# A fused Flamingo block on one core: ternary weights from ScalarE's Sign instead of a clip on VectorE

## The reference, cut to what matters

```
x = x + tanh(g_xattn[0]) * mamba(ctx_1024, layernorm(x))        # selective scan, 16 states
x = x + tanh(g_ffn[0])   * bit_ffn(layernorm(x))                # ternary weights, 512 -> 2048 -> 512
x = x + tanh(g_xattn[1]) * cross_attention(layernorm(x), ctx)   # 16 heads of 128
x = x + tanh(g_ffn[1])   * experts(layernorm(x))                # 4 experts, 512 -> 512 -> 512
```

```
gamma_w = clip(mean(abs(w)), 1e-05, None)
w_dq = clip(round(w / gamma_w), -1.0, 1.0) * gamma_w
```

## Time and profile before

| | us |
|---|---|
| median of 3 runs | 1902.91 |
| lowest, highest | 1902.73, 1903.48 |
| span of the profiled execution | 1906.4 |
| PE busy in it | 1763.0 (92%) |
| DVE busy | 1358.1 (71%) |
| ACT busy | 981.7 (51%) |
| POOL busy | 655.3 (34%) |

### The profile page before, as it was taken

One profiled execution on the slowest core, in us unless ns is written; L12 is line 12 of the kernel. 1 busy time (PEld: TensorE's weight loads), 2 busy tenths in 40 slices (PEclk: granted clock), 3 DMA queues, 4 the chain that ended last, 5 costly groups with the idle time before them and its releaser, 6 DMA issues.

```text
span 1906.4 us, 19429 instructions
## 1 busy us (share of the span) xinstructions
PE 1763.0 (92%) x6054; PEld 803.1 (42%) x6054; DVE 1358.1 (71%) x1963; ACT 981.7 (51%) x1926; POOL 655.3 (34%) x677
## 2 busy tenths in 40 slices
PE   8853999978999999999999999999998989999999
PEld 3321343434444344444443444444444334444543
DVE  2778888899988889989988999897752444431321
ACT  6889665545575455575646465565334333330100
POOL 1222351135565224554632164473202433320100
PEclk9976999989999999999999999999998999999999
DMA  7798992377884115797612368872111699855210
GB/s 256 218 257 232 268 281 71 106 208 186 189 217 121 35 34 127 163 256 198 185 37 54 92 156 234 203 177 78 34 56 45 191 282 268 241 166 214 83 50 34
DMA packets 163175, 300.31 MB, mean 158 GB/s; under 512 B 18937, under 2 KB 51705, under 8 KB 160129
## 3 DMA queue, kind: packets, MB, share of 16 engines
q1 hardware_dynamic: 145792, 236.14, 39.4%
q0 software_dynamic: 17280, 62.92, 16.9%
HBM read 177.64 MB, written 58.33 MB: 124 GB/s over the span
## 4 chain that ended last, share of the span: by engine, by line
PE 64%; DVE 14%; issue 7%; ACT 6%; DMA 4%; POOL 4%; SPq 0%; DVEq 0%; POOLq 0%; ACTq 0%
PE p L781 8%; PE p L792 8%; PE p L758 7%; PE p L741 7%; PE p L828 6%; PE p L634 5%; PE p L720 4%; PE p L715 4%; DVE s_M L957 3%; PE p L843 3%; PE p L764 3%; PE p L681 2%; DVE s_M L952 2%; DVE s_M L962 1%; POOL s_U L1478 1%
## 5 line engine op out<-in xcount | busy, mean ns | idle before, releaser
L957 DVE TENSOR_TENSOR_SCAN s_M<-s_M 128x1024 f32<-128x1024 f32 x128 | 296.7, 2318 | 13.0 <-ACT s_M L1209 10.5
L1100 DVE CUSTOM_DVE_ANT_0 s_U<-p,s_U 128x512 f32<-128x512 f32 x256 | 187.0, 745 | 147.4 <-PE p L758 145.9
L758 PE MATMUL p<-s_U 128*128 128x512 f32 x512 | 268.0, 612 | 4.6 <-DVE s_U L1100 3.4
L1433 POOL DMA_DIRECT2D s_u<-s_M x120 | 112.1, 934 | 463.5 <-DVE s_M L962 418.1
L741 PE MATMUL p<-s_U 128*128 128x512 f32 x512 | 251.8, 600 | 8.3 <-DMA s_U<-in_Wq 3.3
L1478 POOL TENSOR_SCALAR s_U<-s_U 128x512 f32<-128x512 f32 x256 | 242.2, 966 | 6.6
L792 PE MATMUL p<-s_U 128*128 128x512 f32 x512 | 224.3, 593 | 0.0
L781 PE MATMUL p<-s_U 128*128 128x512 f32 x472 | 213.7, 593 | 2.6 <-ACT s_U L1342 2.6
L1209 ACT ACTIVATE s_M<-s_dl,s_small 128x511 f32<-128x511 f32 x256 | 170.4, 716 | 37.2 <-DVE s_M L957 37.1
L1342 ACT COPY s_U<-p 128x512 f32<-128x512 f32 x196 | 105.0, 592 | 162.2 <-PE p L764 160.7
L1337 ACT ACTIVATE s_U<-s_U 128x512 f32<-128x512 f32 x256 | 181.6, 710 | 5.5 <-ACT s_U L1333 0.4
(11 more groups left out here) (178 smaller groups left out, 2424.6 us busy)
## 6 DMA issues: line engine op xcount, KB each, us to landing
s_u<-s_M POOLq DMA_DIRECT2D x120, 512.0 KB, 7.6
s_bc<-bc_scratch SPq DMA_DIRECT2D x128, 256.0 KB, 4.6
k_scratch<-s_U SPq DMA_DIRECT2D x16, 1024.0 KB, 7.0
v_scratch<-s_U SPq DMA_DIRECT2D x16, 1024.0 KB, 4.9
s_U<-in_Wq SPq DMA_DIRECT2D x64, 256.0 KB, 6.9
s_U<-k_scratch SPq DMA_DIRECT2D x64, 256.0 KB, 6.4
s_U<-rk_scratch SPq DMA_DIRECT2D x64, 256.0 KB, 7.0
s_U<-in_Wo SPq DMA_DIRECT2D x64, 256.0 KB, 4.2
```

The lines of the kernel that those rows point to most:

```text
L758: e.matmul(banks[bk][:], qT[j % 3][:, k * 128:(k + 1) * 128], kT[j % 2], start=True, stop=True).then_inc(S["a_s"], 1)
L957: e.tensor_tensor_scan(w, dA[i % 2], w, 0.0, ALU.mult, ALU.add).then_inc(S["m_s"], 1)
L1100: e.tensor_tensor_reduce(out=Pm[j % 2][:, k, :], in0=banks[ABANK[kind, j, k]][:], in1=rkb[j % 2], scale=rq[:, k:k + 1], scalar=-3.0e38, op ...
```

## The change

The `clip` step disappears from the stream Q and from DVE's program, and with it the semaphore `q_cut`. `put` now waits for `rnd` alone and is ACT's Sign function of (rounded value minus MAGIC) in place of a copy of it: the sign of an integer is the integer clipped to -1 and 1. For this the bias has to be a column in memory, `magic`, which POOL fills once at the start; the first `put` waits for that. Nothing else is edited.

```
     for c in range(5):
         QUANT += [("rnd", w, c)] if c < 4 else []
         QUANT += [("put", w, c - 1)] if c else []
-        QUANT += [("clip", w, c)] if c < 4 else []
...
-        elif kind == "clip":
-            out.append(("Q", [("DVE", 1.3)], [(0, "rnd", w, c)], (0, kind, w, c), [], []))
         elif kind == "put":
-            out.append(("Q", [("ACT", 2.0)], [(0, "clip", w, c)], (0, kind, w, c), [], []))
+            out.append(("Q", [("ACT", 2.0)], [(0, "rnd", w, c)], (0, kind, w, c), [], []))
...
+        magic = sb("magic", [128, 1])
...
-                    elif kind == "clip":
-                        e.wait_ge(S["q_rnd"], 4 * w + c + 1)
-                        e.tensor_scalar(stg[c], stg[c], MAGIC - 1.0, MAGIC + 1.0, ALU.max, ALU.min).then_inc(S["q_cut"], 1)
...
-                        e.wait_ge(S["q_cut"], i + 1)
-                        e.activation(dst, stg[c], ACT.Copy, bias=-MAGIC, saturate=False).then_inc(S["q_put"], 1)
+                        e.wait_ge(S["q_rnd"], i + 1)
+                        if i == 0:
+                            e.wait_ge(S["p_set"], 9)
+                        e.activation(dst, stg[c], ACT.Sign, bias=magic[:, 0:1], saturate=False).then_inc(S["q_put"], 1)
...
                 e.memset(raw, 0.0).then_inc(S["p_set"], 1)
+                e.memset(magic[:], -MAGIC).then_inc(S["p_set"], 1)
```

More of the change, by code:

```diff
@@ L26 @@
 SEMS = """
-p_set c_act c_dve q_abs q_sum q_mm q_thr q_cut q_rnd q_put q_raw q_part q_row
+p_set c_act c_dve q_abs q_sum q_mm q_thr q_rnd q_put q_raw q_part q_row
 m_ip m_xp m_dt m_s m_yt m_xs m_u m_xd m_re m_ex m_ln m_da m_z m_ac m_w m_dl m_h0 m_c m_hn m_g m_x m_rv m_rs
```

## The result

The changed kernel is **slower**: 1909.68 us median (1904.82 to 1914.07, 10 runs) against 1902.82 us of the kernel before (1898.53 to 1905.41, 10 runs). The forecast was 1897.9 us, faster, with a range of 1890 to 1905. The kernel went the other way and ended outside the range.

The account below looks back on a forecast made before the run. PE was taken as the bound, with gains in its idle holes: 0 at 191 us, 9.4 at yt, 12.6 at L693, 7.6 at the first head, 4.9 after POOL; 1902.9 - 5.0 = 1897.9 us, range 1890 to 1905.

Parts of the forecast that it names:

- Sign: The put on ACT: a pass of 2007 ns where the copy takes 1908, 1.2 us more over 12, no added table loads.
- The weights' chain: First hole: 1.2 for decays plus 1.2 for Sign less 2.9 for products, taken as 0; PE leaves at 191 us as before.
- DVE in front of yt: Before batch 0's yt: DVE two scan steps further at 4.7 us each, so 9.4 us earlier.
- PE in front of yt: Before yt: products and column sums of K fewer, 13.0 us, less 1.7 behind in K, so PE 11.3 us earlier.
- The second hole: PE's idle time at 400 to 424 us gets filled with K work; L693 comes 12.6 us earlier, near 411 us.
- Four steps to the first head: Turn to first L1100: four whole DVE steps instead of three, 18.9 us; first head at 432.8, 7.6 us earlier.
- POOL: K's sixteenth power starts 14.1 us after K's end, at 425.1, delaying scan transfers; gain falls from 7.6 to 4.9 us.
- rival C: K's power blocks POOL before the first head; each us past 425.1 costs one, slower beyond 430.0, up to 1909 us; chance 0.14.
- D: Norm loads behind K are short, POOL is free in time, the first head's 7.6 us stand: 1895.3 us; chance 0.14.
- A: First hole: weights' chain ends some 5 us later as loads meet more scan transfers, gain is spent: 1902.9 us; chance 0.22.

Follow-up runs that it names:

- wv_first: Changed kernel with the second Wv load, and the store of v behind it, moved on SP ahead of valT's second piece: 1904.29 us, ratio 1.0004 to before.
- both single moves: Changed kernel with s_bc's loads ahead of K's last store of v on SP (ratio 1.0036), or K's last power behind the first head's on POOL (1.0023); together 0.9974.

## Why the prediction was wrong, point by point

- **Sign.** Right. Of the changed kernel's ACT groups by shape (count, busy us, mean ns), the two that answer to the earlier trace rows:

```profile
L1193 ACT ACTIVATE s_wq<-s_U,s_magic 128x2048 fp8e4<-128x2048 f32 x9 | 17.9, 1994 | 0.0
L1186 ACT ACTIVATE s_U<-s_U,s_thr 128x2048 f32<-128x2048 f32 x9 | 17.8, 2003 | 1.0 <-DVE s_thr L876 1.0
```

  1994 ns where 2007 was taken. ACT has 30 table loads, as before, and none stands next to a `put`.
- **The weights' chain, "Sum 0", PE out of the hole at 191 us.** This step failed. The chain was priced on ACT and DVE only, with "the loads shift a little too" for SP. The sum came to 0; measured are 6.5 us at the twelfth `put` and 6.1 at PE's resume (197.26). One shift was not little: PE's Wv moved behind a megabyte of valT. The order shows that swap in one row; the sum had no term for it, although the chain of the earlier trace rows itself has two links through DMA. The swap is not all of it. With Wv ahead again the twelfth `put` comes 129.0 us after the first `rnd` in the mean of seven traces, against 132.5 in the changed kernel and 125.6 in before, so the swap is about half of the 6.9 us there. Of the other half 1.5 us stand between the ninth and the twelfth `put` (13.1 us for 11.6), where the sum had a pair of decays and Sign; the rest stays open.
- **DVE in front of yt, 9.4 us.** Right, but covered. With Wv mended (`wv_first`) the first L990 starts at 273.57 after a wait of 5.93 us for PE, so DVE was there 8.8 us earlier than the 276.43 of before; in the changed kernel 5.2 earlier.
- **PE in front of yt, 11.3 us.** The count of products was right. 6.1 were lost in the hole, and 2.8 between it and yt: 1.1 to waits for weights (2.23 us for Wk, against 1.10 for Wk and Wv in before), and the other 1.7 to slower products, in windows where the granted clock is 0.78 and 0.93 for 0.92 and 1.00 before (191 to 215 and 215 to 240 us). 2.4 were left: yt at 276.55 for 278.94.
- **The second hole.** Right: yt to turn took 142.0 us instead of 144.7, 2.8 less where 12.6 - 9.4 = 3.2 were forecast.
- **Four steps to the first head.** The steps took what they should: 24.2 us from the turn's end, less a wait of 5.3, is the 18.9 of the forecast. This is the second step that failed. The wait for `s_bc` was missing from the sum: it had a term for POOL's queue and none for SP's, though the store of v, the norm loads and `s_bc` stand on it one behind the other.
- **POOL.** The term was right: the last power of K started 14.4 us after K's end (14.1 taken), at 432.94. The K end was 7.5 us later than forecast, so this is rival C's case (power after 430, the head's power after 433). C's price, 4.9 us of gain less 7.8 of delay, gives 2.9 us slower; the first traces stand 3.1 us apart at the ninth row of scores, which is luck in so far as the 5.3 us for `s_bc` are not in that price. And the causes that C named for the delay were others; it came from the first hole. D did not come: the four norm loads landed 6.6 to 9.5 us after their issue. The 2.0 us that the prediction set beside them are given by the Trainium skill (DMA: Bandwidth & Descriptors, "Anatomy of one DMA") for transfers that GpSimd issues, and these are issued by SP; the trace does not agree with them here.
- **The rivals.** A (PE out of the hole after 194) and C both came true by their signs. Whether A's own cause, more scan transfers beside the loads, makes the part of the first hole that the swap leaves open was not tested. They had been treated as cases that exclude each other, each priced alone from the forecast, with 0.14 for slower. They are one chain. The end of K is 7.5 us later than forecast: 6.1 from the first hole and 2.8 behind it, less the 1.9 by which PE was to be ahead of DVE at yt, and 0.4 in the second hole (2.8 for 3.2). That end holds both queues in front of the scan.

## What to carry to other kernels

When a planner moves instructions, read the order of the engine that issues the loads as carefully as those of the engines that compute: for each load that changed places, ask what stands ahead of it in bytes and who waits for it. A wait that two queues cause one behind the other cannot be found by freeing one: both single moves looked worthless or nearly so here, and together they were worth 11 us (from +6.3 to -4.9). And freeing an engine (14.7 us of clips here) gave nothing in one order and 5 us in another, so judge an instruction's price and the order that comes with it by separate kernels.

## What the runs showed of the hardware

**The same short waits cost PE nothing more in one execution, and 5 us in the next.** All kernels here have the same order behind the first heads. Up to 1500 us, the time from one row of scores to the next agrees within 0.7 us in all 20 traces except at four places, near 653, 1006, 1324 and 1425 us; behind 1500 us there are eleven more. Take the first. The windows 650 to 670 us of two traces of the kernel before, `before` and `before_2`, columns as above:

```profile
650.00:670.00 20.00, 17.86 (x61) 5.79 (x60) 10.02 (x17) 9.29 (x17) 0.74 (x2) 0.81 0.15 30
```

```profile
650.00:670.00 20.00, 17.85 (x80) 6.41 (x79) 11.71 (x23) 10.64 (x20) 2.17 (x4) 1.00 0.17 38
```

PE's rows there, in the same two traces: the waits are the same, 1.34 and 0.80 us, and then the same 26 matmul instructions take 3.03, 2.07 and 6.52 us in the one and 1.90, 1.12 and 3.63 in the other, which is 5.0 us in all. The granted clock between 665 and 670 us is 0.50 and 1.00, the lower and the upper level.

```profile
651.82 0.62 PE L673 MATMUL p<-s_identb,s_U 128*128 128x128 bf16 x8 [1.34 <-DVE s_U L999]
660.57 0.69 PE L615 MATMUL p<-s_M,s_dl 16*128 16x512 f32 x1 [0.80 <-ACT s_du L1228]
661.62 3.03 PE L634 MATMUL p<-s_wq,s_U 128*128 128x512 fp8e4 x8
664.58 2.07 PE L615 MATMUL p<-s_M,s_dl 16*128 16x512 f32 x2
666.58 6.52 PE L681 MATMUL p<-s_wq,s_U 128*128 128x512 fp8e4 x16
```

```profile
653.29 0.62 PE L673 MATMUL p<-s_identb,s_U 128*128 128x128 bf16 x8 [1.34 <-DVE s_U L999]
662.03 0.69 PE L615 MATMUL p<-s_M,s_dl 16*128 16x512 f32 x1 [0.80 <-ACT s_du L1228]
663.08 1.90 PE L634 MATMUL p<-s_wq,s_U 128*128 128x512 fp8e4 x8
664.91 1.12 PE L615 MATMUL p<-s_M,s_dl 16*128 16x512 f32 x2
665.97 3.63 PE L681 MATMUL p<-s_wq,s_U 128*128 128x512 fp8e4 x16
```

The eight rows of scores around this place take 91.1 us in two traces of before and 86.1 in the third; of all 20 traces, five (of four kernels) have 91.0 or 91.1, and the others 86.1 to 89.4. What decides between the two is not shown. The second place, near 1006 us, cost 3.3 us in two traces of the changed kernel and in none of the others. All places together, in groups of eight rows, added 5 to 17 us to the shortest groups seen. That is the scatter in the last column of the table, and why two single profiles cannot be compared by their spans.

**The landing time of one load depends on its place in the order.** The four loads of Wv, 512 KB each, landed within 4.5 to 9.1 us of their issue in the first trace of before, and within 4.5 to 16.8 over all traces. The longest, 14.9 to 16.8, are the seven that stand directly behind valT's megabyte on SP. But with valT behind it the same load took up to 14.5 us in the new order, and 11.0 at most in the old, so the megabyte just ahead is one cause among others.
